# Both ends of a fused attention and FFN kernel in another order: where batch 0's copies are issued, what batch 1's copies wait for, and what stands first in the last batch's iteration

## The reference, cut to what matters

```
q, k, v = split(x @ Wqkv + b)                        # 16 heads of 8
s = q @ k^T / sqrt(8), causal;  a = softmax(s)       # 512 x 512 per head
heads 0, 1, 2: a *= 1.6 in one third of the keys each, rows normalised again
x1 = layernorm(x + concat(a @ v) @ Wproj + bproj)
h0 = 2 relu(s0 * [x1, -x1] @ W0)                     # W are +-1 from booleans, 256 -> 512
h1 = 2 relu(s1 * h0 @ W1)                            # 512 -> 512
out = layernorm(x1 + s2 * h1 @ W2)                   # 512 -> 128
```

## Time and profile before

| | us |
|---|---|
| median of 3 runs | 944.77 (943.12 to 948.06) |
| the profiled execution, its own time | 946.07 |
| its span, first to last instruction | 944.3 |
| PE busy | 837.2 (89%) |
| DVE busy | 619.5 (66%) |
| ACT busy | 607.8 (64%) |
| POOL busy | 523.4 (55%) |

### The profile page before, as it was taken

How to read it: one execution, slowest core, us unless ns; L and a number is a source line. 1 busy time by engine, 2 the same in 40 slices (tenths; PEclk the granted TensorE clock), 3 DMA queues, 4 the chain that set the end, 5 groups by cost and what they waited for, 6 DMA issues and landing times.

```text
span 944.3 us, 17048 instructions
## 1 busy us (share of the span) xinstructions
PE 837.2 (89%) x5696; PEld 428.1 (45%) x5696; DVE 619.5 (66%) x2606; ACT 607.8 (64%) x1090; POOL 523.4 (55%) x760
## 2 busy tenths in 40 slices
PE   3257869999999999999999999999999999999855
PEld 1113324545555454545455454545454554544434
DVE  3274848595867768585958677685859586874032
ACT  3104647676777767777777767686776767686823
POOL 1102426575675757575756758575757667484741
PEclk9556979999999999999999999999999999999967
DMA  3655443536354654636363645546363636300000
GB/s 77 66 66 78 53 74 42 69 44 82 42 76 50 75 64 54 76 48 78 46 81 44 76 50 74 63 52 78 46 81 45 76 39 76 40 24 14 12 11 11
DMA packets 66284, 53.16 MB, mean 56 GB/s; under 512 B 4534, under 2 KB 64150, under 8 KB 66198
## 3 DMA queue, kind: packets, MB, share of 16 engines
q1 hardware_dynamic: 65334, 51.30, 43.5%
q10 hardware_dynamic: 864, 0.79, 0.3%
HBM read 9.24 MB, written 4.19 MB: 14 GB/s over the span
## 4 chain that ended last, share of the span: by engine, by line
PE 49%; DVE 12%; ACT 12%; DMA 11%; issue 7%; POOL 6%; SPq 2%; ACTq 0%; POOLq 0%; DVEq 0%
PE av_ps L901 9%; DMA stack<-rowmaxT 8%; PE max_ps L842 8%; PE score_ps L866 7%; PE bank_ps L928 6%; DVE max_ps L681 5%; PE bank_ps L929 5%; ACT e L556 5%; PE bank_ps L825 4%; PE bank_ps L974 3%; POOL res L472 3%; ACT full L548 3%; ACT h_hi L569 3%; DMA stack<-parts 2%; POOL rstd L464 2%
## 5 line engine op out<-in xcount | busy, mean ns | idle before, releaser
L681 DVE CUSTOM_DVE_ANT_0 max_ps<-max_ps,future 128x512 f32<-128x512 f32 (+3 forms) x1024 | 477.8, 517 | 245.4 <-PE max_ps L842 243.1
L556 ACT ACTIVATE e<-score_ps 128x512 f32<-128x512 f32 x640 | 371.0, 613 | 271.0 <-PE score_ps L866 268.9
L842 PE MATMUL max_ps<-stack 72*128 72x512 bf16 (+3 forms) x1024 | 247.7, 312 | 25.6 <-DMA stack<-parts 19.1
L866 PE MATMUL score_ps<-stack 75*128 75x512 bf16 (+3 forms) x1024 | 243.9, 302 | 28.9 <-DMA stack<-rowmaxT 20.9
L436 POOL TENSOR_SCALAR_AFFINE_SELECT e<-e 128x512 f32<-128x512 f32 x256 | 160.1, 637 | 175.7 <-ACT e L556 175.5
L444 POOL TENSOR_TENSOR h_lo<-full,h_hi 128x512 fp32r<-128x512 f32 x120 | 152.8, 1278 | 90.8 <-ACT full L548 90.8
L901 PE MATMUL av_ps<-e,vaug 128*25 128x512 f32 (+3 forms) x2048 | 189.9, 443 | 0.0
L842 PEld LDWEIGHTS max_ps<-stack 72*128 72x128 bf16 x1024 | 81.2, 99 | 160.0 <-issue 81.0
L681 DVE DVE_READ_ACCUMULATOR2_ANT rowmax<- 128x1 f32 x1024 | 143.5, 140 | 0.0
L866 PEld LDWEIGHTS score_ps<-stack 75*128 75x128 bf16 x1024 | 90.9, 98 | 107.7 <-ACT e L556 36.7
L928 PE MATMUL bank_ps<-h_hi,w 128*128 128x512 f32 x256 | 109.3, 427 | 0.2 <-ACT full L548 0.2
(11 more groups left out here) (85 smaller groups left out, 717.3 us busy)
## 6 DMA issues: line engine op xcount, KB each, us to landing
stack<-parts SPq DMA_DIRECT2D x288, 128.0 KB
x_in<-in_L_attn_hidden_states SPq DMA_DIRECT2D x16, 256.0 KB, 16.2
x_res<-in_L_attn_hidden_states SPq DMA_DIRECT2D x16, 256.0 KB, 6.2
out_x<-res SPq DMA_DIRECT2D x16, 256.0 KB, 6.8
stack<-rowmaxT ACTq DMA_DIRECT2D x32, 24.0 KB
e<-in_L_ffn_k SPq DMA_DIRECT2D x1, 256.0 KB, 3.1
e<-in_L_attn_c_attn_w SPq DMA_DIRECT2D x1, 128.0 KB
e<-in_L_ffn_k SPq DMA_DIRECT2D x1, 128.0 KB, 3.0
```

The lines of the kernel that those rows point to most:

```text
L556: nc.scalar.activation(e[g % 2][:, t, :], score_ps[:, t % 2, :], ACT.Exp, scale=SCALE).then_inc(exped, 1)
L681: return nc.vector.tensor_tensor_reduce(out=scored_block, in0=scored_block, in1=future[:, P * (T - 1 - qt):S], scale=1.0, scalar=NEG, op0= ...
L842: return nc.tensor.matmul(out_ap[:, col:col + width], st[0:QK_ROWS, h, 0, P * qt:P * qt + P], st[0:QK_ROWS, h, 1, 0:width], start=True, st ...
L866: return nc.tensor.matmul(out_ap[:, col:col + width], st[0:ALL_ROWS, h, 1, P * kt:P * kt + P], st[0:ALL_ROWS, h, 0, P * kt:S], start=True, ...
```

## The change

It changes the two ends of the pipeline. Iterations 1 to 15 keep their order.

Start: the tiny bias loads go to ACT's queue with a semaphore of their own; DVE waits for Wq and Wk alone and copies them ahead of its clears; PE waits only for that copy; batch 0's subtractions are done for q and for k apart. Of batch 0's 9 copies per half, POOL issues 6 and SP 3. Batch 1's earlier half waits until POOL's copies for batch 0 have landed, and in each of its halves SP issues 3 copies, then waits for `rowmax_in`, the landing of batch 0's rows of maxima of that half, and issues the other 6. Its later half also waits until its earlier half has landed.

End: in iteration 16 a second table holds, with `tok`, `attnT` and `proj` of batch 15 behind `ffn1_2` of batch 14 and ahead of the rest of batch 14's FFN. DVE takes the low part of batch 14's `ffn1_3`, and for batch 15 it does the four normalising instructions of both layernorms in POOL's place; batch 15's first residual lies in `x_in`, so that `res1` stays free for batch 14.

```diff
+PLACES_OF_END = (
+    ("ffn1_2", -2, (0, 0), (0, 1)),
+    ("tok_0", -1, (0, 8), (0, 8)),
+    ("tok_1", -1, (0, 9), (0, 9)),
+    ("attnT", -1, (1, 0), (1, 0)),
+    ("proj", -1, (1, 1), (1, 1)),
+    ("ffn1_3", -2, (1, 2), (1, 2)),
+    ("ffn2T", -2, (1, 3), (1, 6)),
+    ("x1T", -1, (1, 4), (1, 4)),
+    ("ffn0_0", -1, (2, 8), (2, 8)),
+    ("ffn0_1", -1, (2, 9), (2, 9)),
+    ("ffn2", -2, (3, 0), (3, 1)),
+    ("ffn0_2", -1, (3, 0), (3, 1)),
+    ("ffn0_3", -1, (3, 1), (3, 3)),
+    ("ffn1_0", -1, (3, 6), (3, 7)),
+    ("ffn1_1", -1, (3, 8), (3, 9)),
+)
+FFN2_STEPS_OF_END = ((1, 3), (1, 3), (1, 3), (1, 5))
+LAST_SPLIT_OF_END = (1, 3)
+LN_STATS_OF_END = ((1, 2), (3, 4))
+LN_VAR_OF_END = ((1, 2), (3, 5))
+COPIES_OF_POOL = ((1, 0), (1, 1), (0, 2), (2, 0), (2, 1), (2, 2))
+POOL_COPIES_FOR = ((0, 0), (0, 1))
+COPIES_IN_FRONT = 3
...
+        def behind_attention(n):
+            return n.c == B
+        def places(n):
+            return PLACES_OF_END if behind_attention(n) else PLACES
...
+        def wait_stacked(eng, b, half):
+            by_pool = [c for c, h in POOL_COPIES_FOR if h == half and c % 2 == b.parity]
+            copies = 9 * (b.c // 2 + 1) - len(COPIES_OF_POOL) * len(by_pool)
+            eng.wait_ge(stacked[b.parity][half], 16 * copies)
+            if b.c < 2 and by_pool:
+                eng.wait_ge(stacked_by_pool[b.parity][half], 16 * len(COPIES_OF_POOL))
...
+        def res1_of(b):
+            return x_in if last_batch(b) else res1
+        def split_by_dve(b, what):
+            return last_batch(b) or (behind_attention(b + 2) and what == "ffn1_3")
...
             def stack_half(b, half, levels=(0, 1, 2)):
+                pool_does = COPIES_OF_POOL if (b.c, half) in POOL_COPIES_FOR else ()
+                issued = 0
                 for a in range(3):
                     for c in range(3):
                         row = R * (3 * a + c)
-                        if max(a, c) in levels:
+                        if max(a, c) in levels and (a, c) not in pool_does:
+                            if b.c == 1 and issued == COPIES_IN_FRONT:
+                                sp.wait_ge(rowmax_in[half], 16)
+                            issued += 1
...
                 sp.wait_ge(split_step, b.times(3, 3))                  # later_half
+                if b.c == 1:
+                    sp.wait_ge(stacked[b.parity][0], 9 * 16)
...
                     sp.wait_ge(scored, n.times(G * STEPS, 2 * STEPS))  # earlier_half
+                else:
+                    sp.wait_ge(stacked_by_pool[0][1], 16 * len(COPIES_OF_POOL))
...
+            def copies(b, half):                                       # POOL
+                for a, c in COPIES_OF_POOL:
+                    if b.c == 0 and half == 0:
+                        if max(a, c) == 0:
+                            wait_free(pool, use_of(b, "q"))
+                            wait_free(pool, use_of(b, "k"))
+                        else:
+                            pool.wait_ge(split_step, 1 + max(a, c))
+                    row = R * (3 * a + c)
+                    nc.gpsimd.dma_start(stack[b.parity][row:row + R, HALF * half:HALF * half + HALF, :, :],
+                                        parts[b.parity][64 * half:64 * half + 64, c:3 + a + 1:3 + a - c, :]
+                                        ).then_inc(stacked_by_pool[b.parity][half], 16)
...
+            copies(At(0), 0)                                           # POOL, ahead of run(iteration)
+            copies(At(0), 1)
-            pool.wait_ge(w_loaded, 16 * 9)
+            pool.wait_ge(w_loaded, 16 * 4)
...
-            act.wait_ge(w_loaded, 16 * 9)
+            act.wait_ge(bqk_loaded, 16 * 4)
...
-                        if (g, t) == MIDDLE_STEP and live(n + 2):      # ACT
+                        if (g, t) == MIDDLE_STEP and n.c == FIRST:
+                            act.wait_ge(first_rest, 1)
+                            nc.scalar.activation(parts[0][:, 1, :], qk[:, 0, :], ACT.Copy).then_inc(first_middle, 1)
+                            act.wait_ge(split_step, 1)
+                            nc.scalar.activation(parts[0][:, 4, :], qk[:, 1, :], ACT.Copy).then_inc(split_step, 1)
+                        elif (g, t) == MIDDLE_STEP and live(n + 2):
...
-            dve.wait_ge(w_loaded, 16 * 9)
+            dve.wait_ge(wqk_loaded, 16)
...
+                if last_batch(b):                                      # DVE, in layernorm_var
+                    dve.wait_ge(rstd_ready[i], b.times(2, 2))
+                    x = res2 if i else res1_of(b)
+                    for t in range(T):
+                        ins = nc.vector.tensor_scalar(x[:, t, :], x[:, t, :], rstd[:, i, t:t + 1],
+                                                      shift[:, i, t:t + 1], ALU.mult, ALU.add)
+                    ins.then_inc(ln_step[i], 1)
...
             pe.wait_ge(consts_ready, 1)
-            pe.wait_ge(w_loaded, 16 * 9)
-            pe.wait_ge(setup_step, 6)
+            pe.wait_ge(setup_step, 1)
```

More of the change, by code:

```diff
@@ L68 @@
 )
-BANK_USES = tuple((what, batch) for what, batch, _, _ in PLACES)
+PLACES_OF_END = (
[15 more added lines that the diff above has]
+)
+BATCH_OF = {what: batch for what, batch, _, _ in PLACES}
 FFN2_STEPS = ((0, 5), (0, 5), (0, 6), (0, 6))
+FFN2_STEPS_OF_END = ((1, 3), (1, 3), (1, 3), (1, 5))
 SPLIT_STEPS = {"x1T": (2, 6), "ffn0_0": (2, 9), "ffn0_1": (3, 0), "ffn0_2": (3, 2), "ffn0_3": (3, 3),
               "ffn1_0": (3, 7), "ffn1_1": (3, 9), "ffn1_2": (0, 3), "ffn1_3": (0, 4)}
+LAST_SPLIT_OF_END = (1, 3)
 MIDDLE_STEP = (1, 0)
@@ L130, in live @@
         return 0 <= b.c < B
+    def behind_attention(n):
+        return n.c == B
+    def places(n):
+        return PLACES_OF_END if behind_attention(n) else PLACES
     used_before = {FIRST: 0}
     for n in range(FIRST, LAST + 1):
-        used_before[n + 1] = used_before[n] + sum(0 <= n + d < B for _, d in BANK_USES)
+        used_before[n + 1] = used_before[n] + sum(0 <= n + d < B for _, d, _, _ in places(At(n)))
     def use(n, what):
-        before = [d for w, d in BANK_USES[:[w for w, _ in BANK_USES].index(what)]]
+        table = places(n)
+        before = [d for _, d, _, _ in table[:[w for w, _, _, _ in table].index(what)]]
         i = used_before[n.c] + sum(0 <= n.c + d < B for d in before)
@@ L142, in use_of @@
     def use_of(b, what):
-        return use(b + -dict(BANK_USES)[what], what)
+        return use(b + -BATCH_OF[what], what)
     with ExitStack() as ctx:
@@ L229, in block_kernel @@
         split_step = sem("split_step")
+        first_rest = sem("first_rest")
+        first_middle = sem("first_middle")
         stacked = [[sem(f"stacked{i}_half{half}") for half in range(2)] for i in range(2)]
+        stacked_by_pool = [[sem(f"stacked{i}_half{half}_by_pool") for half in range(2)] for i in range(2)]
         v_ready = sem("v_ready")
@@ L280, in last_batch, with split_step_of @@
             return b.c == B - 1
+        def res1_of(b):
+            return x_in if last_batch(b) else res1
+        def split_by_dve(b, what):
+            return last_batch(b) or (behind_attention(b + 2) and what == "ffn1_3")
+        def split_step_of(n, what):
+            return LAST_SPLIT_OF_END if behind_attention(n) and what == "ffn1_3" else SPLIT_STEPS[what]
         def full_slot(b, k):
@@ L289, in _ @@
             sp.dma_start(x_in[:], x_tok[0]).then_inc(x_loaded, 16)
-            sp.dma_start(wqk_in, w_qkv[:, 0:2 * D]).then_inc(w_loaded, 16)
+            sp.dma_start(wqk_in, w_qkv[:, 0:2 * D]).then_inc(wqk_loaded, 16)
             sp.dma_start(wv[:], w_qkv[:, 2 * D:3 * D]).then_inc(w_loaded, 16)
[L292 to L297, removed]
             sp.dma_start(bv[:], b_qkv[2 * D:3 * D].partition_broadcast(P)).then_inc(w_loaded, 16)
@@ L478, in low @@
                     b = n + (-2 if layer and m else -1)
-                    if live(b) and not last_batch(b):
+                    if live(b) and not split_by_dve(b, f"ffn{layer}_{m}"):
                         low_part_by_pool(b, layer, m)
@@ L541, in _ @@
         def _(act):
+            for i in range(2):
+                for half in range(2):
+                    start = D * i + 64 * half
+                    with nc.allow_non_contiguous_dma(reason="64 words"):
+                        nc.scalar.dma_start(bqk[64 * half:64 * half + 64, i:i + 1],
+                                     b_qkv[start:start + 64].rearrange("(h r) -> r h", r=R)).then_inc(bqk_loaded, 16)
             act.wait_ge(consts_ready, 1)
             nc.scalar.activation(exp_one[:], ident[0:1, 0:1], ACT.Exp)
-            act.wait_ge(w_loaded, 16 * 9)
+            act.wait_ge(bqk_loaded, 16 * 4)
             def take(u, out_ap, func, **kw):
@@ L593, in iteration @@
                                 sums_out(n, 0)
-                        for what, d, _, step in PLACES:
+                        for what, d, _, step in places(n):
                             b = n + d
@@ L609, in iteration @@
```

(18 more changed lines are left out.)

39 lines of the change are left out of this document (25 added, 14 removed).

## The result

| | before | after |
|---|---|---|
| median | 945.33 (942.42 to 951.93, 9 runs) | 938.66 (934.8 to 941.1, 9 runs) |
| ratio, 95% interval | | 0.9923 (0.9898 to 0.9949) |
| profiled execution, and its span | 946.07, 944.3 | 936.0, 934.2 |

The kernel is faster by 7.3 us (4.8 to 9.6), where 21.6 were forecast. The time 938.66 lies outside the range of 914 to 937.

The account below looks back on a forecast made before the run. DMAs were taken to bound the start, and a one-batch chain of engines waiting in turn the end. Gains of 17 plus 4.6, 21.6 from 946.07, gave 924.5, or 923 against the median; range 914 to 937.

Parts of the forecast that it names:

- T0: Start: batch 0's first maxima begin at 28 instead of 39.76, with POOL issuing six of nine copies.
- S0: Start: the first scores begin at 52.5 instead of 75.69, a gain of 23.2.
- S1: Start of batch 1's scores: 104.9 instead of 124.07, a gain of 19.2.
- the end's gain: End, batches 14 and 15: earlier last sums and DVE's normalising, less work moved in between, give 4.6, bounds 1 and 8.
- Part of that is given back: Start: batch 1's other six copies are issued only at S0, so PE stalls 2.7 for that half.
- Their wait: Batch 1's rows of maxima, issued at 92.8 in front of a full queue of nine, wait 12.07 to land.
- (b): Rival: rows of maxima wait for all nine outstanding copies; S1 is 115, start gains 9, time 931; chance 0.15.
- (a): Rival: POOL's queue adds no bandwidth; T0 is 34.9, start is worth 7, time 933; chance 0.14.
- (c): Rival: POOL's copies are issue bound and land two at a time; T0 24.5, time 918; chance 0.08.
- (d): Rival: writing descriptors occupies POOL so long that the start waits; slower, 959 at 5 us per issue; chance 0.08.
- (e): Rival: the end is worth nothing because of the slow clock; 928, its chance included in the forecast's 0.50.
- cover: Start: batch 1's first three copies end at 48, before ACT issues the rows of maxima at 49.4; 1 us to spare.

Follow-up runs that it names:

- e2: The kernel before with only the change's end added: 940.08 us, ratio 0.9945 (0.9926 to 0.9964) to before.
- e3: The changed kernel with COPIES_IN_FRONT 9 instead of 3, so no copy of batch 1 is held: 926.32 us, ratio 0.9809 to before.

## Why the prediction was wrong

| step | forecast | after |
|---|---|---|
| PE's first transposes | 6.0 | 4.86 |
| low parts of q and k | 15.5 | 15.3 |
| POOL's price for a copy | 1.2 | 0.72 |
| first maxima, T0 | 28 | 33.4 |
| rows of maxima, wait | 3.1 | 2.81 |
| first scores, S0 | 52.5 | 57.5 |
| **PE waits for batch 1's earlier half** | **2.7** | **6.12** |
| **PE waits for batch 1's later half** | **0** | **6.01** |
| batch 1's rows issued | S0 + 40.3 | S0 + 51.3 |
| their wait | 12.07 | 11.54 |
| batch 1's scores, S1 | 104.9 | 120.4 |
| the end's gain | 4.6 | 5.2 (e2) |

**The step that failed is "Part of that is given back".** It put what holding batch 1's copies costs at a single stall of PE, 2.7. The trace has two of 6. For the earlier half, the six held copies took 15.7 us from the landing of the rows, where I had 14.3; and PE wanted them at S0 + 9.5, not 11.65: the row I took that from, at 87.34 in the earlier trace rows, was itself late by a wait for DVE of 1.71, in its brackets, which PE didn't have this time. For the later half I worked out when its copies end (92.1), but never set that against when PE wants them. PE's timeline of before has that tile, with no wait of its own:

```profile
107.05 0.38 PE L842 MATMUL max_ps<-stack 72*128 72x512 bf16 x1
```

That is 31.2 after the first score (75.82), so in the prediction's own sum PE wants the later half at 52.5 + 31.2 + 2.7 = 86.4, and a stall of 5.7 stands there at nothing, without a reason. The run has 6.01: PE wants the half at 94.9 and gets it at 100.9. Of the 8.8 us between 92.1 and 100.9, 5 are the later S0; the rest is the first stall and the slower copies, passed on through the second rows to the second six. A hold makes a loop: rows, copies, PE, rows, and each lateness goes round. From the first score to the issue of batch 1's rows the two stalls are 12.1 of the 13.8 us that it takes longer than before; the other 1.6 fit the clock, which fell again for 10.2 and 6.8 us in that stretch, where before it fell for 3.4, but no run tests that. Two more us are lost on the way to batch 2, whose rows are issued at 164.90 against 166.61: the 3.7 us gained at S1 have shrunk to 1.7. So S1 came 15.5 us later than forecast: 5 by the late first maxima and 11 in the stretch in which the hold works.

e3 is the check: the same kernel without the hold has no such stall and lies at 926.3, inside the range and 3 us from the forecast. That nearness doesn't confirm the sum: e3's first maxima came at 35.3 and its S1 at 111.5, 6.6 after the forecast's.

**T0** was mis-sized by 5.4. I let POOL's six copies run at one queue's rate of 2.16 each; from POOL's first issue at 15.23 to the first maxima they took 18.1. The rate was not the mistake. By the packets of the trace of after, POOL's queue had moved as much as six copies by 27.3 and as much as nine by 32.0. But the last piece of the earlier half's six landed at 33.2, so about three copies' worth of the later half went through before the earlier one was complete; SP's three of the earlier half were in at 24.0. I had taken the queue to finish its copies in the order in which they were issued. No run holds POOL's own later six back, so what that would give is not shown.

**Their wait** is near the forecast (11.54, 12.07) by luck. The forecast had nine copies outstanding when batch 1's rows were issued. By the packets, about five were at 108.78, with the load of `x_res` issued in the same moment, and the rows landed only when all five had. That is what rival (b) says of such rows, so (b) is not excluded: with nine outstanding the wait could have been longer.

**Rivals.** (a), no bandwidth from a second queue, is out for SP and POOL: 119 GB/s against 60. The Trainium skill's rule that spreading DMAs over issuing engines gives none ("DMA: Bandwidth & Descriptors", "Rules for kernel authors") does not hold for these copies on SP and POOL; for SP and ACT no run decides it. The same page's rule on which engines a copy with 8 partitions uses, in "Why a DMA increments its semaphore by 16 and not by 1", the trace agrees with as far as a share can tell: 0.60 for SP and ACT, 0.98 with POOL. (c) is out with T0 at 33.4, (d) with 0.72 per issue, (e) with e2. None of the rivals was the hold itself. I had it as cover with 1 us to spare, and asked what it protects (the rows), not whom it delays.

**The end** was right in sum, 5.2 (3.4 to 7.0) against 4.6. Of its terms, DVE's normalising took 1.12 against POOL's 1.76 (0.88 forecast); from the landing of the last rows of maxima to the end of the last sums it took 34.3 us before and 29.5 after, 4.8 less (4.3 forecast). The others were not measured one by one.

## What to carry to other kernels

A wait that holds back bulk copies for an urgent small one has to be priced at both ends: what the small one saves (4.6 us here) and when the held ones are wanted (two stalls of 6). An idle queue is a hint to look, not the price: with six let through instead of three the queue still went idle, and the 10 us were back. For each consumer of a moved transfer, put its landing against the time it is wanted, and take that time from a row without a wait of its own. Don't count on a queue to finish its copies in the order of issue.

## What was not expected of the hardware

Copies of 128 KB into 8 partitions moved at 60 GB/s in one window of SP's queue alone (share 0.57), and SP's queue alone reached 85 in another (0.56). With ACT's queue beside it they moved at 77 (87 with the load of x, share 0.60), and with POOL's at 111 (119 with it, 0.98). POOL issues one in 0.72 us, nearly as cheap as SP with room (0.67 in the earlier trace rows); ACT's twelve took 1.39 each. On POOL's queue the first six were complete only when as much as nine copies had been moved.
